# A GNN kernel's dense stage: two instruction blocks change place, one in TensorE's stream and one in ScalarE's

## The reference, cut to what matters

```python
h = max(layernorm(x), 0)
x = x + L0(h)          # message passing with an edge MLP, then a node MLP
h = max(layernorm(x), 0)
x = x + L1(h)          # graph attention, 8 heads of 32

# L0, after agg = segment_sum(...) over 100000 edges, 6250 nodes:
h = (1 + eps) * x + agg                          # 6250 x 256
h = relu(_ln(h @ w1 + b1, g1, be1))              # 256 -> 1024
h = relu(_ln(h @ w2 + b2, g2, be2))              # 1024 -> 1024
y = h @ w3 + b3                                  # 1024 -> 256
out = relu(_ln(x + y, bn_g, bn_b))
# _ln: (x - mean) * rsqrt(var + 1e-5) * g + b
```

## Time and profile before

| | |
|---|---|
| median of 3 runs | 4217.17 us (4206.21 to 4219.63) |
| the profiled execution's own time | 4245.11 us |
| its span in the profile | 4243.3 us |
| PE, DVE, ACT, POOL busy over the span | 65%, 58%, 33%, 47% |
| the dense stage in the span | about 1660 to 2785 us |

### The profile page before, as it was taken

One profiled execution on the slowest core, in us unless ns is written; L12 is line 12 of the kernel. 1 busy time (PEld: TensorE's weight loads), 2 busy tenths in 40 slices (PEclk: granted clock), 3 DMA queues, 4 the chain that ended last, 5 costly groups with the idle time before them and its releaser, 6 DMA issues. The chain is left out here.

```text
span 4243.3 us, 86741 instructions
## 1 busy us (share of the span) xinstructions
PE 2741.7 (65%) x25602; PEld 2350.9 (55%) x25603; DVE 2441.3 (58%) x5647; ACT 1418.1 (33%) x3617; POOL 2001.3 (47%) x2147
## 2 busy tenths in 40 slices
PE   0056565666666665899999999836554666666663
PEld 0045555555545455888888888824443444444442
DVE  3545555555555553566666666645545555566566
ACT  1522222222222232677777777611100111111110
POOL 0245554555555552333333333335545555565554
PEclk9977787788777777999999999956667777777766
DMA  5333333333333332011100110034434444444443
GB/s 158 123 103 103 109 108 102 111 106 111 106 108 105 104 111 66 20 30 30 30 30 30 30 30 30 28 98 123 120 104 118 112 130 129 127 133 132 127 128 102
DMA packets 203584, 393.32 MB, mean 93 GB/s; under 512 B 45288, under 2 KB 98028, under 8 KB 202900
## 3 DMA queue, kind: packets, MB, share of 16 engines
q0 software_dynamic: 75552, 209.66, 18.1%
q1 hardware_dynamic: 125750, 182.11, 14.1%
q10 hardware_dynamic: 2222, 0.87, 0.1%
HBM read 360.28 MB, written 32.20 MB: 92 GB/s over the span
## 5 line engine op out<-in xcount | busy, mean ns | idle before, releaser
L522 POOL DMA_INDIRECT rows<-tab_scratch,idx x784 | 768.8, 981 | 675.4 <-POOLq L520 438.9
L1474 POOL DMA_INDIRECT a_rows<-tab_scratch,a_srcs x784 | 772.1, 985 | 614.3 <-PEq L1579 399.5
L1539 PE MATMUL sum_ps<-feat,a_hot 128*125 128x264 f32 x1960 | 709.8, 527 | 421.3 <-PEq L1578 287.2
L1539 PEld LDWEIGHTS sum_ps<-feat,a_hot 128*125 128x125 f32 x1960 | 485.1, 258 | 551.5 <-issue 440.6
L948 PE MATMUL z_ps<-ah,w2h 128*128 128x125 f16 x3200 | 543.3, 220 | 0.8 <-PEq L1020 0.6
L948 PE MATMUL z_ps<-ah,w2l 128*128 128x125 f16 x3200 | 543.2, 218 | 0.0
L948 PE MATMUL z_ps<-al,w2h 128*128 128x125 f16 x3200 | 543.2, 217 | 0.0
L549 ACT ACTIVATE rh<-mlp_ps 128x1024 f16<-128x1024 f32 x196 | 200.7, 1024 | 907.2 <-ACTq L548 729.6
L569 PE MATMUL sum_ps<-rows,hot 128*125 128x256 f16 x980 | 325.8, 332 | 272.8 <-issue 127.6
L562 PE MATMUL mlp_ps<-ewa,eab 128*128 128x256 f16 x788 | 230.7, 318 | 403.0 <-PEq L558 343.8
L1486 ACT ACTIVATE feat<-d 128x32 f32<-128x32 f32 x196 | 45.0, 229 | 1230.7 <-ACTq L1485 833.4
(11 more groups left out here) (214 smaller groups left out, 6455.6 us busy)
## 6 DMA issues: line engine op xcount, KB each, us to landing
ea<-edge_t SPq DMA_DIRECT2D x394, 128.0 KB
dstb<-dst_flat SPq DMA_DIRECT2D x196, 256.0 KB
rows<-tab_scratch,idx POOLq DMA_INDIRECT x784
a_rows<-tab_scratch,a_srcs POOLq DMA_INDIRECT x784
tab_scratch<-prow SPq DMA_DIRECT2D x50, 128.9 KB
acc<-x SPq DMA_DIRECT2D x5, 1250.0 KB
h_scratch<-h SPq DMA_DIRECT2D x10, 625.0 KB
tab_scratch<-tb SPq DMA_DIRECT2D x10, 625.0 KB
```

What stands on the lines that cost most here:

```text
L522: pool.indirect_dma_start(rows[:, s, k, :], None, dram["tab0"], bass.IndirectOffsetOnAxis(ap=idx[:, s, k:k + 1], axis=0),).then_inc(rows_r ...
L1474: pool.indirect_dma_start(rows[:, b % RING, k, :], None, dram["tab1"], bass.IndirectOffsetOnAxis(ap=srcs[:, c:c + 1], axis=0),).then_inc(r ...
L1539: ins = pe.matmul(out[:], hot[:, h, k, :], feat[:, row, k, :], start=(k == 0), stop=(k == CB - 1))
```

## The change

On TensorE, `make_h(i + 1)` and `turn(i + 2)` go ahead of the output layer of tile i-2, which is no longer in two halves. On ScalarE, `squares` goes ahead of `row_deviation(0)` and `deviation(1)`. No instruction is added or removed.

```diff
@@ tensor @@
-                if has(i, 2):
-
-                    pe.wait_ge(a_split[1], 1)
-                    pe.sem_inc(a_split[1], -1)
-                    pe.wait_ge(y_free, 1)
-                    pe.sem_inc(y_free, -1)
-                    output(range(KH // 2))
                 if has(i, 0, 1):
                     make_h(i + 1, 1 - p)
                 if has(i, 0, 2):
                     turn(i + 2, p)
                 if has(i, 2):
-                    output(range(KH // 2, KH)).then_inc(y_done, 1)
+
+                    pe.wait_ge(a_split[1], 1)
+                    pe.sem_inc(a_split[1], -1)
+                    pe.wait_ge(y_free, 1)
+                    pe.sem_inc(y_free, -1)
+                    output(range(KH)).then_inc(y_done, 1)
@@ scalar @@
                     biased(0, "b1", 0)
                     biased(0, "b1", 1)
+                if has(i, 0):
+                    squares()
                 if has(i, 3):
                     row_deviation(0)
                 if has(i, 2):
                     deviation(1)
-                if has(i, 0):
-                    squares()
                 if has(i, 4):
```

## The result

| | before | changed |
|---|---|---|
| median of 10 runs | 4218.11 us (4206.21 to 4226.75) | 4237.09 us (4224.02 to 4251.97) |
| profiled execution: time, span | 4245.11, 4243.3 us | 4251.13, 4249.3 us |
| dense stage: first to last of the 50 `squares` | 1042.8 us | 1058.7 us |

The ratio is 1.005 with an interval of 1.003 to 1.007: 19 us slower (13 to 30). The forecast was 4227 us, +10, in a range of 4203 to 4250.

A forecast was written before the change was run, and what follows sets the result against it. A ring from layer 1 over ScalarE, GpSimd and VectorE back to layer 1 bounds the kernel. TensorE's part 0, ScalarE's part +0.21 us a body, 47 times, +9.9 us: 4227 us, range 4203 to 4250.

The forecast's parts named there:

- The bound: Layer 1, `biased(0)`, `squares`, GpSimd, VectorE `x1` to `low_h`, next layer 1: one turn is the 21.45 us period.
- TensorE's part: Early `make_h` and undivided output layer: worth 0 us a body, with bounds of -1.11 and +0.1.
- Rival A: Early `make_h` counts: wait at layer 1 shrinks by 1.11 us a body, 53 us in all, 4164; chance 0.07.
- The squares' gain: ScalarE's `squares` start right behind the biased tile, at 2012.17 instead of 2012.37: 0.20 us earlier.
- The order at the ports: After 887, GpSimd's 888 goes 0.06 us ahead of VectorE's product and runs free at 0.63 us; the product follows.
- The sum: `x1` 0.21 us late, all serial from there: 47 bodies x 0.21 = +9.9 us, 4227 on the median.
- Rival B: Squares' gain counts, roots' delay is hidden: -0.20 x 47 = -9.4 us, 4208; product done by 7.7; chance 0.11.
- Rival C: VectorE's reciprocal for `scaled(1)` is blocked by 887 too: +0.70 us a body, 33 us in all, 4250; chance 0.12.
- Rival D: All of `deviation(1)`'s delay shows: +1.16 x 47 = +55 us, 4272; chance 0.04.
- The wait at layer 1: TensorE's wait for `h_split` ahead of layer 1, 1.11 us, would grow to about 1.3 us.

The follow-up runs named there:

- low_h_first: Kernel before with VectorE's `low_h` ahead of the `st` copy: 3531.82 against 3542.62 us, ratio 0.9972.
- row_norm_first: Kernel before with the row norm ahead of the norm of layer 2 in all three streams, `deviation(1)` ahead of `squares`: 3521.3 against 3543.8 us, ratio 0.9936.
- te_only: Kernel before with only TensorE's stream of the changed kernel: 3542.68 against 3542.62 us, ratio 1.0002.
- late_variance: Kernel before with TensorE's `variance(0)` a quarter of layer 2's second half later: 3556.93 against 3541.87 us, ratio 1.0038.
- all four kernels: Kernel before, the changed one, and two edits of the former: `squares` between the two roots (ratio 1.0012); `deviation(1)` first, then `squares`, `row_deviation(0)` (0.9989).
- row_norm_low_h: Kernel before with the row norm ahead of layer 2's norm in all three streams and `low_h` ahead of the `st` copy: 3524.63 against 3543.8 us, ratio 0.9942.

## Why the prediction was right, step by step

**The bound: right.** The ring over layer 1, `squares`, GpSimd, `x1` and `low_h` sets the period. `low_h_first` and `row_norm_first` each took work out of it and gained; on TensorE's side alone `te_only` left the stage as it was (1042.5 us) and `late_variance` made it longer.

**TensorE's part, 0: right.** `te_only` moved the time by 0.1 us. Rival A is dead: `high_h` waits for ScalarE's turn.

**The squares' gain, 0.20 us: wrong, it was 0.09.** Measured from layer 1, `squares` started at 4.40 and now start at 4.31, not 4.20. I had taken ScalarE's wait for its own previous result from `activated(1)` to `high(1)`, 0.12 us. Behind the biased activation it is 0.21 us: 2011.87, where the four parts end at 2010.52 + 1.13 = 2011.65 (the row says 0.21). Everything behind inherits that.

**The order at the ports: right.** The last column is the predicted place plus the 0.11 us above.

| us from layer 1 | predicted | measured | with the late squares |
|---|---|---|---|
| 887 starts | 5.43 | 5.52 | 5.54 |
| 888 starts, takes | 6.85, 0.63 | 6.94, 0.63 | 6.96 |
| product starts | 6.91 | 7.01 | 7.02 |
| product ends | 8.54 | 8.62 | 8.65 |
| 889 ends | 8.81 | 8.89 | 8.92 |
| `row_norm` ends | 9.17 | 9.26 | 9.28 |
| 907 ends | 11.03 | 11.15 | 11.14 |
| `x1` later by | 0.21 | 0.33 | 0.32 |

888 was first by 0.07 us, where 0.06 were predicted, and no step deviates by more than 0.03 us from the last column.

By the Trainium skill's rule (SBUF - State Buffer, section "SBUF: two separate sides") whoever starts first keeps the shared ports to its end. The trace agrees for the product and the folding additions in all four kernels, with the starts 0.07 to 0.13 us apart. For the row norm at 2024.99 it does not, as long as the recorded start is taken for the moment that counts.

The forecast of this order was partly luck: it hung on 0.06 us, less than the 0.11 us by which the squares' gain was wrong, and held because that error moved the product and 888 alike. By the prediction's own working the other order would have cost about the same.

**The sum.** 0.21 + 0.11 = 0.32 us a body, x 47 = 15.0 us, against 15.9 us of stage and 19 us (13 to 30) in the medians. The term that was mis-sized is the squares' gain, 5.2 us in all. Spacing by spacing the trace says the same: without the one that holds the dip the changed kernel's last 46 average 21.68 us against 21.37, 0.31 us a body or 14.4 us, and the dip adds 1.4 us, a cost that the sum did not have. What is left to the 19 us is within the interval.

**Rival B** (only the gain shows) is dead: the product ended at 8.62, not by 7.7. **Rival C** (the reciprocal is blocked) too: it ran from 2013.49 to 2014.43, 0.83 us of that beside 887 (2013.08 to 2014.32), and took the same 0.94 us as before. **Rival D** (the whole 1.16 us show): the idle time ahead of `low(1)` is still 0.35 us.

**The wait at layer 1** was to be 1.3 us and is 1.9 in the body shown (1.67 on average, where it was 1.03). I added the 0.2 us to the old 1.11 and forgot that TensorE's idle time is a sum: its matmuls take some 19.6 us a body in either kernel (551.5 and 545.9 of 600 us). `variance(0)` now waits 0.35 us instead of some 0.65, since the squares come earlier against it, and what isn't waited there is waited at layer 1. It did not touch the time. The body shown is 21.87 us and the one in front 21.45, both somewhat longer than their stage's means of 21.61 and 21.28; spacing from body to body varies by such amounts, so means, not single bodies, belong in a comparison.

**Later misses.** For `low_h_first` I started from a body in which VectorE's work ahead of `low_h` took longer than on average (the norm of line 1251 0.88 us, held by GpSimd's line 911, where the mean is 0.755), and so saw more to gain than the stage as a whole had. For `row_norm_low_h` I added gains on one wait that only one of them could take.

## What to carry to other kernels

When no engine is busy all the time, follow the wait of the busiest one round until it closes: the ring's steps are the only ones that count, and two cuts that shorten the same wait don't add. Starting a shared resource's user earlier gains nothing if the other user's input is made late by it: here 0.09 us for one engine cost 1.26 us for the other, of which 0.33 showed. Cut the ring first and cover the waits inside the body next: the second alone made the stage 9.3 us longer here, with stretches at half clock, and on top of the first 45.7 us shorter.

## What the hardware showed unexpectedly

- A blocked instruction's duration in the trace holds its wait. The product (1.20 us free) ends 1.05 or 1.06 us after its blocker, 888 (0.63) 0.48 or 0.49 and 889 (0.40) 0.27, so each ends 0.13 to 0.15 us sooner than its free duration after the blocker's end. For the row norm of line 1249 (0.41) it is 0.14 (2025.96 against 2025.82), 0.27 us sooner. What those parts are no run shows.
- Which of two instructions is held can hang on some 0.1 us, and the recorded start does not always tell which: a lead of 0.07 us was enough for line 888, and one of 0.10 us was not for the row norm.
- A reciprocal of 128x125 fp32 is not held by a GpSimd addition (0.94 us with and without one beside it), while the product of two SBUF inputs is.
- ScalarE's wait for its own previous write is not one number: 0.12 us lie between `activated(1)` and `high(1)`, 0.21 us between the biased activation and `squares`. Both the writer and the reader differ between the two, and which of them matters was not tried.
- With TensorE's idle time in one wait a body (1.80 us on average) the clock was halved 8 times in 50 bodies; with 1.03 and 0.67 us apart in the kernel before it was not, and with 1.67 and 0.28 in the changed one it was once (all behind the first three bodies). Where TensorE's idle time lies can thus be a cost of its own.
